# Residual rows issued by ScalarE, the output projection placed after the last attention slot, and transposing loads spread out, in an attention and FFN layer on 8 cores

## The chip, the cores and the metric

The kernel is one program on all 8 cores of one Trainium2 chip. Time is device microseconds (us) of the slowest core. Each core has the matrix engine (TensorE, PE in the profile), VectorE (DVE), ScalarE (ACT), GpSimd (POOL) and SyncE (SP), which each run their own instruction stream in order, and issue DMAs in that same order. They meet by semaphores.

## The reference

For 4 sequences of 4096 tokens and 2048 features, two post-norm steps (cut to what matters):

```python
# attention: tokens of a sequence are seen as 2 batches of 2048, 16 heads of 128
mixed = x @ Wqkv.T                       # q, k, v
attn = softmax((q @ k.T) / sqrt(128))
out = (attn @ v) @ Wproj.T + bproj
x = layernorm(x + out)                   # called h1 in the kernel
# feed-forward: weights packed in 4 bits, with a scale for each group of 128 inputs
gate, up = x @ w_gate.T, x @ w_up.T
y = (silu(gate) * up) @ w_down.T
x = layernorm(x + y / sqrt(mean(y * y) + 1e-6))
```

## The kernel before

Each core computes 2048 output tokens of one sequence, in 16 tiles of 128 tokens.

Attention runs in 8 slots of 128 steps. In a step TensorE computes the scores of 256 keys for 512 queries (`pe_scores`, 2 matmuls of 512 columns), ScalarE exponentiates them (`act_exp`, one instruction of 1024 columns), and TensorE multiplies an earlier result with V (`pe_context`, 8 matmuls of 129 columns). Every 16 steps VectorE normalizes and evacuates the context (`dve_ctx_evac`), during which the next context matmul waits. Between scores and context `pe_program` puts filler: in slots 0 to 6 five projection matmuls' worth of the next slot, and in slot 7, from step `OC_FIRST = 60` on, five matmuls of the output projection (`pe_out_proj`). The rest of the output projection follows behind attention.

The output projection has 64 groups (16 tiles by 4 blocks of 512 columns) of 16 matmuls. Group q is written to one of two PSUM banks, and waits for VectorE's evacuation of group q-2. The work on a tile goes round several engines:

- SP loads the tile's context transposed (`sp_ctx_load`) and the residual rows `xr` (`sp_xr_load`, 1 MB, two buffers: tile t+2 takes the buffer of tile t).
- POOL adds the bias to `xr` (`pool_bias`), VectorE adds `xr` to the projection for each group, with statistics (`dve_post_norm`: `r`, `statB`, `aggB`), POOL turns the variance into `rstdB` (`pool_rstd_b`), and VectorE writes `h1f`.
- POOL stores `h1f`, ScalarE casts it to `h1b` (`act_h1_cast`) and stores that.

POOL's stream is written out in a fixed order, which the change leaves alone:

```python
    for tile in range(TILES):
        pool_rstd_b(g, S, M, tile)
        g.wait_ge(S.h1_done, tile + 1)
        g.dma_start(out=M.d_h1[tile * 128:(tile + 1) * 128, :],
                    in_=M.h1f[tile % 2][:]).then_inc(S.h1_stored[tile % 2], 16)
        if tile + 2 < TILES:
            pool_bias(g, S, M, tile + 2)
```

The feed-forward part takes 4 chunks of 512 tokens. A chunk has 44 gate/up operations (`pe_gate_up`, 32 matmuls each) on transposed `h1T`, and 4 x 11 blocks of the down projection. SP feeds it: `sp_wgu_load` fetches weights into a ring of 4 (1 MB each; the load of operation k waits until operation k-4 is done), and at operation 10 of a chunk `sp_h1t_load` fetches the next chunk's four tiles with four transposing loads in a row.

Of the kernel before, what the change touches and what calls it, by code (L numbers as in the profile page):

```python
# [543 lines left out]
def act_program(a, S, M, exact):  # L544
    a.wait_ge(S.consts, 1)
    g = 0
    while g < GROUPS:
        act_proj_evac(a, S, M, g)
        g += 1
    tile = 0  # L550
    for n in range(SLOTS * STEPS):
        act_exp(a, S, M, n)
        last = n % STEPS == STEPS - 1
        while g < groups_done(n if exact and last else n - 1):
            act_proj_evac(a, S, M, g)
            g += 1
        if n >= (SLOTS - 1) * STEPS and 4 * (tile + 1) <= oc_groups_done(n % STEPS - 5):
            act_h1_cast(a, S, M, tile)
            tile += 1
    while tile < TILES:  # L560
        act_h1_cast(a, S, M, tile)
        tile += 1

    for ch in range(FCH):
        for op in range(GU_OPS):
            act_silu(a, S, M, ch * GU_OPS + op)
        for oc in range(4 if ch + 1 < FCH else 3):
# [4 lines left out]
    a.wait_ge(S.l_norm, 12)
    a.wait_ge(S.l_done, 4)
    a.dma_start(out=M.d_out[r * 128:(r + 1) * 128, 1024:2048],
                in_=M.res[3][:, 1024:2048]).then_inc(S.out_last[1], 16)
# [525 lines left out]
                          ).then_inc(S.ctxt_in[tile % CTXT_RING], 16)  # L1101


def sp_xr_load(y, S, M, tile):
    if tile >= 2:
        y.wait_ge(S.oc_evac, 4 * (tile - 1))
    y.dma_start(out=M.xr[tile % 2][:],
                in_=M.d_xrows[tile * 128:(tile + 1) * 128, :]).then_inc(S.xr_in[tile % 2], 16)


def sp_h1t_load(y, S, M, ch, tiles):
    if ch >= 2:
# [27 lines left out]
def sp_program(y, S, M, exact):  # L1140
# [10 lines left out]
    if exact:  # L1151
        sp_row_max(y, S, M, SLOTS - 1)
    y.wait_ge(S.pv_done, (SLOTS - 1) * STEPS)
    sp_xr_load(y, S, M, 0)
    sp_xr_load(y, S, M, 1)
    xr = ctxt = 0
    for i in range(STEPS):
        if i % 16 == 15:
            sp_ctx_store(y, S, M, (SLOTS - 1) * QBLOCKS + i // 16)
        if i == 34:  # L1160
            y.wait_ge(S.proj_done, SLOTS * GROUPS)
            while ctxt < CTXT_RING:
                sp_ctx_load(y, S, M, ctxt)
                ctxt += 1
        if 4 * (xr + 1) <= oc_groups_done(i - 2):
            sp_xr_load(y, S, M, xr + 2)
            xr += 1
        while ctxt - CTXT_RING < xr and 32 * (ctxt // 4 + 1) <= i:
            sp_ctx_load(y, S, M, ctxt)
            ctxt += 1  # L1170
    y.wait_ge(S.pv_done, SLOTS * STEPS)
    for j in range(2):
        y.wait_ge(S.ctx_stored[j], 16 * (SLOTS * QBLOCKS // 2))
    while xr + 2 < TILES:
        if xr == TILES - 5:
            sp_wgu_load(y, S, M, 0)
            sp_wgu_load(y, S, M, 1)
        if xr >= TILES - 4:
            sp_h1t_load(y, S, M, 0, range(2 * (xr - TILES + 4), 2 * (xr - TILES + 4) + 2))
        while ctxt < TILES and ctxt - CTXT_RING <= xr:  # L1180
            sp_ctx_load(y, S, M, ctxt)
            ctxt += 1
        sp_xr_load(y, S, M, xr + 2)
        xr += 1
    sp_wgu_load(y, S, M, 2)
    sp_wgu_load(y, S, M, 3)
    for ch in range(FCH):
        for op in range(GU_OPS):
            kc = ch * GU_OPS + op + WGU_RING
            if kc < FCH * GU_OPS:  # L1190
                sp_wgu_load(y, S, M, kc)
            if op == 10 and ch + 1 < FCH:
                sp_h1t_load(y, S, M, ch + 1, range(4))
            if op == 34 and ch == 0:
                for du in range(WD_RING):
                    sp_wd_load(y, S, M, du)
# [157 lines left out]
```

## Time and profile before

| what | us |
| --- | --- |
| median of 3 runs (lowest, highest) | 4144.91 (4142.04, 4147.2) |
| the profiled execution, time | 4153.74 |
| its span (slowest core, core 2) | 4152.0 |
| spans of all cores | 4127.6 to 4152.0 |
| TensorE busy in the span | 4060.1 (98%) |
| mean granted TensorE clock of the cores | 0.996 to 0.999 |

The profile is of one execution, on its slowest core. Rows of a timeline give start, duration, engine, line and operation; in brackets stands the idle time before the instruction and what ended it. Rows with SPq, ACTq or POOLq, and POOL's DMA rows, are the issue of a DMA, not its transfer.

### The profile page before, as it was taken

The page shows a single profiled execution, that of the slowest core. Times are in us where ns is not written, and L with a number is a line of the kernel's source. Part 1 is how long each engine was busy: PE and PEld are TensorE (multiplying, and loading weights), DVE is VectorE, ACT ScalarE, POOL GpSimd, SP SyncE. Part 2 cuts the span into 40 slices and gives each one's busy share as a digit, 9 for nine tenths or more (in the row PEclk, how much of TensorE's full clock was granted, in tenths as well). Part 3 has the DMA queues.
Part 4 walks back from the last instruction along what each step waited for, and adds up shares of the span by engine and source line. Part 5 has one row for each costly group of instructions (what it writes and reads, how often), then busy time and mean ns, then how long its engine had stood idle before and what let it go on. Part 6 is the DMA issues. An engine that isn't in the chain of part 4 may idle for free.

```text
span 4152.0 us, 66120 instructions; the slowest of 8 cores (4127.6 to 4152.0 us)
## 1 busy us (share of the span) xinstructions
PE 4060.1 (98%) x26491; PEld 2296.5 (55%) x26881; DVE 948.6 (23%) x1433; ACT 1400.2 (34%) x1610; POOL 286.4 (7%) x434
## 2 busy tenths in 40 slices
PE   7999999999999999999999999999999999999998
PEld 4666666666666766666554444444444444444443
DVE  0054452222222223220234100022100300022124
ACT  1355555555555555557642100000000000000001
POOL 1100000000000000000223000000000000000000
PEclk9999999999999999999999999999999999999999
DMA  9777776465655655656459545447444654446433
GB/s 146 130 172 169 178 165 126 107 137 121 124 119 118 140 104 120 135 119 111 110 157 261 191 167 199 159 155 231 152 157 152 201 189 152 157 164 216 162 127 123
DMA packets 251041, 635.65 MB, mean 153 GB/s; under 512 B 115184, under 2 KB 137712, under 8 KB 212720
## 3 DMA queue, kind: packets, MB, share of 16 engines
q1 hardware_dynamic: 202496, 426.29, 31.6%
q0 software_dynamic: 45792, 196.10, 25.5%
q10 hardware_dynamic: 2448, 8.91, 0.5%
q8 instruction: 225, 3.69, 0.4%
q14 instruction: 80, 0.66, 0.0%
HBM read 643.83 MB, written 119.54 MB: 184 GB/s over the span
## 4 chain that ended last, share of the span: by engine, by line
PE 93%; SPq 2%; DMA 2%; issue 1%; ACT 1%; DVE 0%; POOL 0%; ACTq 0%; DVEq 0%; POOLq 0%
PE pJ L283 16%; PE pC L339 11%; PE pJ L269 11%; PE pS L320 10%; PE pS L412 7%; PE pS L393 7%; PE pS L389 7%; PE pC L389 4%; PE pJ L393 3%; PE pC L393 3%; PE pJ L389 3%; PE pJ L361 3%; PE pC L412 3%; PE pJ L412 3%; SPq L1118 2%
## 5 line engine op out<-in xcount | busy, mean ns | idle before, releaser
L496 ACT ACTIVATE P<-pS 128x1024 bf16<-128x1024 f32 x1024 | 1027.8, 1026 | 356.8 <-PE pS L320 342.6
L283 PE MATMUL pJ<-x,wq 128*128 128x512 bf16 x2984 | 756.9, 381 | 28.5 <-DMA x<-xc 23.8
L339 PEld LDWEIGHTS pC<-V,P 128*128 128x128 bf16 x8192 | 549.8, 98 | 168.0 <-issue 11.3
L339 PE MATMUL pC<-V,P 128*128 128x129 bf16 x8192 | 634.0, 220 | 3.6 <-DVE ctxg L613 3.1
L320 PE MATMUL pS<-Q,K 128*128 128x512 bf16 x1829 | 561.7, 379 | 18.9 <-ACT P L496 7.5
L269 PE MATMUL pJ<-wq,x 128*128 128x256 bf16 x4096 | 514.8, 273 | 0.4
L283 PEld LDWEIGHTS pJ<-x,wq 128*128 128x128 bf16 x3072 | 301.0, 98 | 381.9 <-issue 33.4
L269 PEld LDWEIGHTS pJ<-wq,x 128*128 128x128 bf16 x4096 | 400.7, 98 | 134.8
L609 DVE RECIPROCAL rcp<-pC 128x4 f32<-128x4 f32 x64 | 11.7, 183 | 1477.9 <-PE pC L339 1477.9
L393 PE MATMUL pS<-h1T,wgu 128*128 128x512 bf16 x1408 | 318.3, 379 | 0.0
L389 PE MATMUL pS<-h1T,wgu 128*128 128x512 bf16 x1408 | 318.3, 379 | 0.0
L412 PE MATMUL pS<-wd,hffnT 128*128 128x512 bf16 x1380 | 303.1, 379 | 1.5
L905 POOL DMA_DIRECT2D x<-xc x256 | 138.3, 558 | 1743.6 <-PE pJ L283 1089.0
L361 PE MATMUL pJ<-wp,ctxT 128*128 128x512 bf16 x1001 | 232.8, 380 | 9.1 <-DVE r L674 7.8
L517 ACT ACTIVATE sg<-pS 128x512 bf16<-128x512 f32 x88 | 52.4, 597 | 532.5 <-PE pS L389 532.5
L389 PEld LDWEIGHTS pS<-h1T,wgu 128*128 128x128 bf16 x1408 | 137.9, 98 | 166.0
L412 PEld LDWEIGHTS pS<-wd,hffnT 128*128 128x128 bf16 x1408 | 137.8, 98 | 166.1
L393 PEld LDWEIGHTS pS<-h1T,wgu 128*128 128x128 bf16 x1408 | 137.8, 98 | 166.1
L389 PE MATMUL pC<-h1T,wgu 128*128 128x512 bf16 x704 | 163.5, 386 | 13.5 <-DMA wgu<-wgu_scr 13.5
L695 DVE TENSOR_TENSOR hffnT<-sg,pS 128x512 bf16<-128x512 bf16 x88 | 60.6, 688 | 498.6 <-PE pS L393 492.1
L361 PEld LDWEIGHTS pJ<-wp,ctxT 128*128 128x128 bf16 x1024 | 100.0, 98 | 129.7 <-issue 11.4
L320 PEld LDWEIGHTS pS<-Q,K 128*128 128x128 bf16 x2048 | 157.0, 98 | 11.5 <-issue 8.4
(107 smaller groups left out, 2647.8 us busy)
## 6 DMA issues: line engine op xcount, KB each, us to landing
wgu<-wgu_scr SPq DMA_DIRECT2D x176, 1024.0 KB, 4.9
x<-xc POOLq DMA_DIRECT2D x256, 512.0 KB, 12.4
wd<-wdn_scr SPq DMA_DIRECT2D x174, 512.0 KB, 3.5
wgu_scr<-bits SPq DMA_DIRECT2D x44, 1024.0 KB, 5.1
wdn_scr<-bits SPq DMA_DIRECT2D x44, 512.0 KB, 4.6
xr<-xrows SPq DMA_DIRECT2D x16, 1024.0 KB, 7.1
h_scr<-h1f POOLq DMA_DIRECT2D x16, 1024.0 KB, 7.1
res<-h_scr POOLq DMA_DIRECT2D x16, 1024.0 KB, 8.9
```

What stands on the lines that cost most here:

```text
L269: mm = t.matmul(out[:, tt * 256:(tt + 1) * 256], x[:, hc, (2 * h + tt) * 128:(2 * h + tt + 1) * 128], M.wq[:, pair, 1, hc, :], start=(hc = ...
L283: mm = t.matmul(out, M.wq[:, pair, part, hc, h * 128:(h + 1) * 128], x[:, hc, :], start=(hc == 0), stop=(hc == HC - 1))
L320: mm = t.matmul(M.pS[n % 2][:, h * 512:(h + 1) * 512], M.K[s % 2][:, l, kt * 128:(kt + 1) * 128], M.Q[s % 2][:, l, qc * 512:(qc + 1) * 512 ...
L339: mm = t.matmul(M.pC[:, o:o + 129], M.P[n % 3][:, h * 512 + qt * 128:h * 512 + (qt + 1) * 128], M.V[s % 2][:, 2 * p + h, l, :], start=(p = ...
L361: mm = t.matmul(M.bank(6 + q % 2), M.ctxT[tile % CTXT_RING][:, hc, :], M.wp[2 * oc + hc // 8][:, hc % 8, :], start=(hc == 0), stop=(hc == ...
L389: mm = t.matmul(M.bank(b), w[:, kt % 4, kt // 4, 0:128], M.h1T[ch % 2][:, :, kt, :], start=(kt == 0), stop=(kt == HC - 1))
L393: mm = t.matmul(M.bank(b + 1), w[:, kt % 4, kt // 4, 128:256], M.h1T[ch % 2][:, :, kt, :], start=(kt == 0), stop=(kt == HC - 1))
L412: mm = t.matmul(M.bank((oc % 2) * 4 + tt), M.hffnT[:, 4 * ut + j, tt * 128:(tt + 1) * 128], M.wd[du % WD_RING][:, j, :], start=(ut == 0 an ...
L496: a.activation(out=M.P[n % 3][:], in_=M.pS[n % 2][:], func=AF.Exp, bias=0.0, scale=NORM).then_inc(S.exp_done, 1)
L695: v.tensor_tensor(out=M.hffnT[:, kc % GU_OPS, :], in0=M.sg[kc % 2][:], in1=M.bank(PAIR_BANKS[kc % 4] + 1), op=ALU.mult).then_inc(S.h_done, 1)
L905: g.dma_start(out=M.x[gc % 2][:, 4 * q:4 * q + 4, :], in_=M.d_x[w, ch, :, 4 * q:4 * q + 4, :]).then_inc(S.x_in[(gc % 2) * 4 + q], 16)
L1118: y.dma_start_transpose(out=M.h1T[ch % 2][:, tt, :, :], in_=M.d_h1b[tile * 128:(tile + 1) * 128, :]).then_inc(S.h1t_in[ch % 2], 16)
```

## The change

Four edits:

- `OC_FIRST` becomes 128, so slot 7 has no filler and all 64 groups of the output projection follow attention.
- The residual rows of tiles 2 to 15 are no longer issued by SP but by ScalarE, at the end of `act_h1_cast` of the tile two before.
- The cast of `h1b` is four instructions of 512 columns in place of one of 2048.
- The four transposing loads of the next chunk's `h1T` are issued at operations 8, 15, 22 and 29, one each, in place of four at operation 10.

```diff
-OC_FIRST = 60
+OC_FIRST = STEPS
...
+H1T_OPS = (8, 15, 22, 29)
...
-def act_h1_cast(a, S, M, tile):
+def act_h1_cast(a, S, M, k):
...
+    tile, ut = divmod(k, 4)
+    cols = slice(512 * ut, 512 * (ut + 1))
     a.wait_ge(S.h1_done, tile + 1)
     if tile >= 2:
         a.wait_ge(S.h1b_stored[tile % 2], 16 * (tile // 2))
-    a.copy(out=M.h1b[tile % 2][:].rearrange("t (u j p) -> t u j p", u=4, j=4),
-           in_=M.h1f[tile % 2][:].rearrange("t (u p j) -> t u j p", u=4, j=4)
-           ).then_inc(S.h1b_done, 1)
+    cast = a.copy(out=M.h1b[tile % 2][:, cols].rearrange("t (j p) -> t j p", j=4),
+                  in_=M.h1f[tile % 2][:, cols].rearrange("t (p j) -> t j p", j=4))
+    if ut < 3:
+        return
+    cast.then_inc(S.h1b_done, 1)
     a.wait_ge(S.h1b_done, tile + 1)
     a.dma_start(out=M.d_h1b[tile * 128:(tile + 1) * 128, :],
                 in_=M.h1b[tile % 2][:]).then_inc(S.h1b_stored[tile % 2], 16)
+    if tile + 2 < TILES:
+        a.wait_ge(S.oc_evac, 4 * (tile + 1))
+        a.dma_start(out=M.xr[tile % 2][:], in_=M.d_xrows[(tile + 2) * 128:(tile + 3) * 128, :]
+                    ).then_inc(S.xr_in[tile % 2], 16)
...
-        if n >= (SLOTS - 1) * STEPS and 4 * (tile + 1) <= oc_groups_done(n % STEPS - 5):
-            act_h1_cast(a, S, M, tile)
-            tile += 1
-    while tile < TILES:
-        act_h1_cast(a, S, M, tile)
-        tile += 1
+        if n >= (SLOTS - 1) * STEPS and 4 * (k // 4 + 1) <= oc_groups_done(n % STEPS - 5):
+            act_h1_cast(a, S, M, k)
+            k += 1
+    for k in range(k, 4 * TILES):
+        act_h1_cast(a, S, M, k)
...
-def sp_xr_load(y, S, M, tile):
-    if tile >= 2:
-        y.wait_ge(S.oc_evac, 4 * (tile - 1))
-    y.dma_start(out=M.xr[tile % 2][:],
-                in_=M.d_xrows[tile * 128:(tile + 1) * 128, :]).then_inc(S.xr_in[tile % 2], 16)
...
-            if op == 10 and ch + 1 < FCH:
-                sp_h1t_load(y, S, M, ch + 1, range(4))
+            if op in H1T_OPS and ch + 1 < FCH:
+                tt = H1T_OPS.index(op)
+                sp_h1t_load(y, S, M, ch + 1, range(tt, tt + 1))
```

TensorE's stream in slot 7, before (a step late in the slot; pS are scores, pC the context, pJ the output projection):

```order
L339 MATMUL pC<-V_100,P_140 128x129 x8
L320 MATMUL pS<-Q_102,K_98 128x512 x2
L361 MATMUL pJ<-wp_82,ctxT_83 128x512 x5
L339 MATMUL pC<-V_100,P_141 128x129 x8
L320 MATMUL pS<-Q_102,K_98 128x512 x2
L361 MATMUL pJ<-wp_75,ctxT_84 128x512 x5
```

And changed, at the end of the slot:

```order
L321 MATMUL pS<-Q_102,K_98 128x512 x2
L340 MATMUL pC<-V_100,P_140 128x129 x8
L340 MATMUL pC<-V_100,P_141 128x129 x8
L340 MATMUL pC<-V_100,P_139 128x129 x8
L362 MATMUL pJ<-wp_75,ctxT_83 128x512 x8
L362 MATMUL pJ<-wp_76,ctxT_83 128x512 x8
L362 MATMUL pJ<-wp_77,ctxT_83 128x512 x8
```

The pJ matmuls are gone from between scores and context; the first of them follows the last context matmuls.

ScalarE's stream behind attention, before (P is the last exponential, h1b the cast rows):

```order
L496 ACTIVATE P_139<-pS 128x1024
L505 CAST h1b_123<-h1f_106 128x2048
L509 DMA h1b_scr<-h1b_123 128x2048
L505 CAST h1b_124<-h1f_107 128x2048
L509 DMA h1b_scr<-h1b_124 128x2048
```

Changed:

```order
L497 ACTIVATE P_139<-pS 128x1024
L509 CAST h1b_123<-h1f_106 128x512 x4
L515 DMA h1b_scr<-h1b_123 128x2048
L519 DMA xr_103<-xrows 128x2048
L509 CAST h1b_124<-h1f_107 128x512 x4
L515 DMA h1b_scr<-h1b_124 128x2048
L519 DMA xr_104<-xrows 128x2048
```

Each residual load now stands behind the four casts and the store of the tile two before it.

SP's stream near the end of the output projection, before (ctxT and h1T are transposing loads, wgu the first weights of the feed-forward part):

```order
L1107 DMA xr_103<-xrows 128x2048
L1126 DMA wgu_112<-wgu_scr 128x4096
L1126 DMA wgu_113<-wgu_scr 128x4096
L1099 DMA_TRANSPOSE ctxT_86<-ctx_scr 128x16x128
L1107 DMA xr_104<-xrows 128x2048
L1118 DMA_TRANSPOSE h1T_126<-h1b_scr 128x16x128 x2
L1107 DMA xr_103<-xrows 128x2048
L1118 DMA_TRANSPOSE h1T_126<-h1b_scr 128x16x128 x2
L1107 DMA xr_104<-xrows 128x2048
```

Changed:

```order
L1108 DMA_TRANSPOSE ctxT_85<-ctx_scr 128x16x128
L1128 DMA wgu_112<-wgu_scr 128x4096
L1128 DMA wgu_113<-wgu_scr 128x4096
L1108 DMA_TRANSPOSE ctxT_86<-ctx_scr 128x16x128
L1120 DMA_TRANSPOSE h1T_126<-h1b_scr 128x16x128 x4
L1128 DMA wgu_114<-wgu_scr 128x4096
L1128 DMA wgu_115<-wgu_scr 128x4096
```

The residual loads are gone from SP, and the four transposing loads of the first chunk stand together. The streams of POOL and VectorE have the same instructions in the same order around the output projection in both kernels.

## Rows read from the trace of the kernel before

**Rows 1.** Timeline, VectorE in slot 7: start, duration, what [idle before, releaser].
```profile
1937.73 0.18 DVE L609 RECIPROCAL rcp<-pC 128x4 f32<-128x4 f32 x1 [30.64 <-PE pC L339]
...
1954.13 0.18 DVE L609 RECIPROCAL rcp<-pC 128x4 f32<-128x4 f32 x1 [15.41 <-PE pC L339]
...
1986.37 0.18 DVE L609 RECIPROCAL rcp<-pC 128x4 f32<-128x4 f32 x1 [15.14 <-PE pC L339]
...
2138.38 0.18 DVE L609 RECIPROCAL rcp<-pC 128x4 f32<-128x4 f32 x1 [2.94 <-PE pC L339]
```

**Rows 2.** Busy time (x count) of PE, PEld, DVE, ACT, POOL; clock; DMA share; GB/s.
```profile
2139.30:2295.40 156.10, 147.48 (x668) 66.50 (x680) 76.35 (x112) 39.23 (x11) 57.42 (x40) 0.99 0.79 234
```

**Rows 3.** Timeline, TensorE at the end of the output projection.
```profile
2287.11 2.72 PE L361 MATMUL pJ<-wp,ctxT 128*128 128x512 bf16 x6 [3.29 <-DVE r L674]
2289.99 5.56 PE L361 MATMUL pJ<-wp,ctxT 128*128 128x512 bf16 x25 [0.17 <-issue]
2295.39 3.62 PE L389 MATMUL pS<-h1T,wgu 128*128 128x512 bf16 x16
```

**Rows 4.** The chain that ended last, one transfer: start, duration.
```profile
2269.55 9.54 DMA xr<-xrows
```

**Rows 5.** Timeline, POOL near the end of the output projection.
```profile
2279.23 4.50 POOL L918 TENSOR_TENSOR xr<-xr,bias 128x2048 f32<-128x2048 f32 x1 [9.94 <-DMA xr<-xrows]
2283.71 0.22 POOL L928 TENSOR_SCALAR epsB<-aggB 128x1 f32<-128x1 f32 x1
```

**Rows 6.** Timeline, VectorE behind attention.
```profile
2147.90 0.69 DVE L674 TENSOR_TENSOR r<-pJ,xr 128x512 f32<-128x512 f32 x1 [1.99 <-PE pJ L361]
...
2151.09 1.34 DVE L687 TENSOR_SCALAR h1f<-r,aggB,rstdB 128x2048 f32<-128x2048 f32 x1 [1.33 <-POOL rstdB L931]
...
2284.75 1.34 DVE L687 TENSOR_SCALAR h1f<-r,aggB,rstdB 128x2048 f32<-128x2048 f32 x1 [5.87 <-POOL rstdB L931]
```

**Rows 7.** Timeline, TensorE in chunks 1 and 2 of the feed-forward part.
```profile
2847.92 3.62 PE L389 MATMUL pJ<-h1T,wgu 128*128 128x512 bf16 x16
2851.37 3.62 PE L393 MATMUL pJ<-h1T,wgu 128*128 128x512 bf16 x16
2862.06 5.93 PE L389 MATMUL pC<-h1T,wgu 128*128 128x512 bf16 x16 [7.07 <-DMA wgu<-wgu_scr]
2867.83 3.62 PE L393 MATMUL pC<-h1T,wgu 128*128 128x512 bf16 x16
...
3326.85 5.65 PE L389 MATMUL pC<-h1T,wgu 128*128 128x512 bf16 x16 [6.47 <-DMA wgu<-wgu_scr]
```

**Rows 8.** Timeline, SP's issues behind attention and in chunk 1.
```profile
2233.26 6.24 SPq L1099 DMA_TRANSPOSE ctxT<-ctx_scr  x1
...
2827.96 22.47 SPq L1118 DMA_TRANSPOSE h1T<-h1b_scr  x4
```

**Rows 9.** Timeline, TensorE in slot 7 behind a cast on ScalarE.
```profile
2035.66 0.59 PE L320 MATMUL pS<-Q,K 128*128 128x512 bf16 x2 [1.34 <-ACT P L496]
```

**Rows 10.** Timeline, ScalarE behind attention.
```profile
2152.57 3.90 ACT L505 CAST h1b<-h1f 128x2048 bf16<-128x2048 f32 x1 [13.08 <-DVE h1f L687]
2156.55 0.34 ACTq L509 DMA_DIRECT2D h1b_scr<-h1b  x1
```

**Rows 11.** Tile xr within slot 7 (1990 to 2140).
```profile
DMA to landing us min/median/max: 5.2/5.4/5.4
```

**Rows 12.** Tile xr behind attention (2140 to 2300).
```profile
DMA to landing us min/median/max: 6.4/7.8/9.7
```

**Rows 13.** DMA issues from 2820 to 2870: KB each, median us to landing.
```profile
wgu<-wgu_scr SPq DMA_DIRECT2D x6, 1024.0 KB, 12.4
```

**Rows 14.** What line L389 waited for on core 7: us, times.
```profile
  DMA wgu<-wgu_scr: 3.8, 1
```

**Rows 15.** Spans and mean granted clock, two of the cores.
```profile
core 2: 4152.0 us, clock 0.996
...
core 7: 4139.8 us, clock 0.998
```

More of the change, by code:

```diff
@@ L549, in act_program @@
         g += 1
-    tile = 0
+    k = 0
     for n in range(SLOTS * STEPS):
@@ L1153, in sp_program @@
     y.wait_ge(S.pv_done, (SLOTS - 1) * STEPS)
-    sp_xr_load(y, S, M, 0)
-    sp_xr_load(y, S, M, 1)
-    xr = ctxt = 0
+    for tile in range(2):
+        y.dma_start(out=M.xr[tile][:],
+                    in_=M.d_xrows[tile * 128:(tile + 1) * 128, :]).then_inc(S.xr_in[tile], 16)
+    done = ctxt = 0
     for i in range(STEPS):
@@ L1164, in sp_program @@
                 ctxt += 1
[L1165 to L1168, printed above, removed]
+        if 4 * (done + 1) <= oc_groups_done(i - 2):
+            done += 1
+        while ctxt - CTXT_RING < done and 32 * (ctxt // 4 + 1) <= i:
             sp_ctx_load(y, S, M, ctxt)
@@ L1173, in sp_program @@
         y.wait_ge(S.ctx_stored[j], 16 * (SLOTS * QBLOCKS // 2))
-    while xr + 2 < TILES:
-        if xr == TILES - 5:
+    for tile in range(done, TILES - 2):
+        if tile == TILES - 5:
             sp_wgu_load(y, S, M, 0)
             sp_wgu_load(y, S, M, 1)
-        if xr >= TILES - 4:
-            sp_h1t_load(y, S, M, 0, range(2 * (xr - TILES + 4), 2 * (xr - TILES + 4) + 2))
-        while ctxt < TILES and ctxt - CTXT_RING <= xr:
+        if tile >= TILES - 4:
+            tt = 2 * (tile - TILES + 4)
+            sp_h1t_load(y, S, M, 0, range(tt, tt + 2))
+        while ctxt < TILES and ctxt - CTXT_RING <= tile:
             sp_ctx_load(y, S, M, ctxt)
             ctxt += 1
-        sp_xr_load(y, S, M, xr + 2)
-        xr += 1
     sp_wgu_load(y, S, M, 2)
```

## The prediction

> **What bounds the kernel now.** The busy times say TensorE, nearly everywhere. So I read the list of waits only to find where TensorE waits, and then timelines there. Three places matter. In slot 7 before the filler begins, ScalarE's exponentials set the pace: VectorE's context evacuations, one for every 16 steps, stand 16.40 us and then 32.24 / 2 = 16.12 us apart [rows 1], about 1.007 us a step. Behind attention TensorE is busy 147.5 of 156.1 us [rows 2]; the rest is three waits for VectorE, the last one 3.29 us [rows 3]. That one goes back to residual rows that landed late: the load took 9.54 us [rows 4], POOL stood idle 9.94 us for it [rows 5], and VectorE then waited 5.87 us for POOL's rstdB [rows 6]. In the feed-forward part core 2 waits twice for weights, 7.07 and 6.47 us [rows 7], behind four transposing loads that hold SP for 22.47 us [rows 8].
>
> **Part 1, filler out of slot 7.** From the first evacuation of the slot to the last it takes 2138.38 - 1937.73 = 200.65 us [rows 1]. Without filler all eight stretches go at ScalarE's pace: 16.40 + 7 x 16.12 = 129.24 us. Attention ends 71.4 us earlier, near 2066.8. This holds already that ScalarE no longer stops for casts between exponentials, each of which cost TensorE at least the 1.34 us of [rows 9] and happened four times.
>
> All 64 groups now follow. A group is 16 matmuls of 512 columns; 16 such matmuls follow the last 16 after 2851.37 - 2847.92 = 3.45 us when nothing waits [rows 7], so unhindered they take 64 x 3.45 = 221 us and end at 2287.8, against 2295.4 now [rows 3]: 7.6 us earlier. This is the best that Parts 1 and 2 could give.
>
> **Part 2, residual rows behind the cast.** This is where I expect the loss. The load of xr for tile t+2 used to need only the evacuation of tile t's last group, and SP's queue; now it stands behind h1f of tile t and four casts on ScalarE. And POOL's stream has the bias addition of tile t+2 ahead of rstdB of tile t+1. POOL works in order: at 2283.71 epsB starts the moment the bias addition ends, and VectorE's h1f follows [rows 5, 6]. Before, that was a wait now and then. In the changed kernel it closes a loop of one tile: h1f(t), cast, load of xr(t+2), bias(t+2), rstdB(t+1), h1f(t+1). Its length L, from start of h1f to start of the next h1f:
>
> - start of h1f to start of the cast: 2152.57 - 2151.09 = 1.48 us [rows 6, 10];
> - the cast, 3.90 us [rows 10]; in four pieces I take 4.2. Four pieces do not exist before. From below it is 3.9; from above I allow another 0.3 us a piece, 5.1; I stay close to the row, since the elements are the same;
> - to the issue of xr: 0.08 + 0.34 for the h1b store [rows 10] + 0.08 = 0.50 us;
> - D, the load from issue to landing, see below;
> - landing (2269.55 + 9.54 = 2279.09) to bias start 0.14 us [rows 4, 5];
> - bias start to h1f start: 2284.75 - 2279.23 = 5.52 us [rows 5, 6].
>
> L = 11.84 + D. The loop hides behind TensorE only if it is no longer than a tile's 4 x 3.45 = 13.8 us, that is with D under 2.0 us. D was 5.2 to 5.4 us with little traffic [rows 11] and 6.4 to 9.7 us behind attention [rows 12]. Those are the two ends, 5.2 and 9.7. In the change the transposing load that preceded xr in SP's queue (6.24 us of issue, [rows 8]) no longer precedes it, but the h1b store, half as large as xr, does; a store of h1f is in flight too. I take 6.5 us: 5.2 plus a quarter, for half as many bytes ahead of which part is done in the time of the issue. So L = 18.3 us, 4.5 us longer than a tile.
>
> The rows say that the load slowed from 5.4 to 7.8 us in the median when other traffic grew, both times in SP's queue [rows 11, 12]. The Trainium skill says the same in "DMA: Bandwidth & Descriptors", section "Issuing engines are not separate DMA queues": DMAs started by different engines run on the same 16 DMA engines and interleave, so another issuer saves only issue time. That rule speaks against this edit: it would not let D fall under the 5.2 us of a quiet stretch (about 4170 in all), while a queue with transfers of its own would. No run so far shows this load on ScalarE's queue.
>
> Now the sum. The first tile ends 13.8 us after 2066.8, at 2080.6. h1f(0) starts 2151.09 - 2147.90 = 3.2 us later [rows 6], at 2083.8. The loop turns 14 times (loads of tiles 2 to 15): 14 x 18.34 = 256.8, so h1f(14) starts at 2340.6. The last two loads meet the feed-forward weights and the four transposing loads that now stand together on SP; the load in such a stretch took 9.54 us [rows 4]. I add 3 and 2 us: 2345.6. TensorE restarts 2287.11 - 2284.75 = 2.36 us after h1f's start and does two groups in 2295.39 - 2287.11 = 8.28 us [rows 3, 6]; that is 1.4 us over 2 x 3.45, as the first matmuls after a wait run at the lower clock. The output projection ends at 2356.2, against 2295.4: **60.8 us later**. In the other turns these 1.4 to 2.3 us at the lower clock [rows 3, 7] fit into the 4.5 us that TensorE is ahead of the loop, and cost nothing. The casts are ahead of nothing else on ScalarE.
>
> **Part 3, transposing loads spread.** Matmul group starts are 2867.83 - 2851.37 = 16.46 us apart across the first wait where 6.9 is normal: 9.6 us, of which 2.3 are the lower clock. The second: 6.47 + (5.65 - 3.62) = 8.5 us [rows 7]. Together 18.1 us on core 2. One transposing load alone takes about 22.47 / 4 = 5.6 us of SP [rows 8]. A weight load is issued four operations ahead, so three operations, 20.7 us, cover it; 5.6 us leave 15 of them, more than a load needed even in the crowd (the median of the weight loads there was 12.4 us [rows 13]). So these waits go. On core 7 there is only one wait, 3.8 us [rows 14], perhaps 5 with the clock. If cover were gone, a late load costs what it costs now.
>
> **Sum.** Core 2: 4152.0 + 60.8 - 18.1 = 4194.7. Core 7: 4139.8 + 60.8 - 5 = 4195.6 [rows 15]. Both are near 4195, and with the 1.7 us outside the span of the profiled execution 4197. The runs' median is 8.8 us below the profiled one, which had core 2's long waits; core 7 alone would give 4139.8 + 1.7 = 4141.5 [rows 15]. On the median: 4144.9 + 60.8 - 18.1 = 4187.6, or with core 7's gain 4200.7. I take **4193**.
>
> **Rivals.**
>
> A. *The residual chain has two tiles of time, not one.* xr has two buffers, and the load serves tile t+2. Were it not for POOL's order, the chain would only need to bring xr(t+2) in time for its first group: 3.2 + 1.48 + 4.2 + 0.5 + 6.5 + 0.14 + 4.5 + 0.7 = 21.2 us after tile t's last group, where 6 groups, 20.7 us, are free. TensorE would wait about 0.5 us per pair of tiles, 4 us in all, and the change gives -7.6 + 4 - 5 to -18.1: **about 4130, faster**. It decides from the point where rstdB(t+1) does not wait for xr(t+2). Against it: epsB right behind the bias addition [rows 5].
>
> B. *The loop turns faster*, D = 5.2, as in a quiet stretch: 14 x 1.3 + 5 = 23 us less, 4170. For it: traffic per us falls as tiles take longer. Against: h1b's store directly ahead.
>
> C. *The load is slow throughout*, D near 9.7: 14 x 3.2 less the 5 already counted, about 40 us more, 4233. For it: the maximum of [rows 12] on an ordinary tile. Against: it needs transposing loads in front each time.
>
> D. *Spreading does not stop the waits for weights.* One transposing load among fast-running loads still delays one. The 5 to 18 us are then not gained: 4198 to 4211.
>
> **How the numbers follow.** My forecast, the loop at L of 17.8 to 19.5 us, 58%, by itself 4183 to 4210. A 6%, B 18%, C 8%, D together with the loop 10%. The range 4163 to 4225 holds B, the forecast and D, and leaves out A and C. A measurement of this kernel tells a change from none at about 0.2%, 8 us. Faster: A alone, 0.06; the same, the tail of B in which D is near 4 us, 0.02; slower 0.92.
>
> **What would show it.** Right: VectorE's h1f starts 18 to 19 us apart behind attention, TensorE waits for `r` about 4.5 us in nearly every tile, POOL waits for xr in every tile and epsB starts at the end of the bias addition; slot 7 takes about 129 us; no wait of TensorE for wgu. Wrong: h1f starts 13.8 us apart, or POOL's waits for xr ending before aggB is there. The sum fails in proportion if D is not 6.5 us: each us is 14 us of time.

## The result, and the profile after

| what | predicted | measured |
| --- | --- | --- |
| ratio to before | 1.0116 (4193) | 1.0158 [1.0135, 1.0181] |
| time, us | 4193 (4163 to 4225) | 4144.91 x 1.0158 = 4210; runs of 4205.6 to 4212.7 |

The change makes the kernel slower by 1.6%, 65 us where I had forecast 48. The profiled execution (core 1, span 4488.1 us) had a granted TensorE clock of 0.81 to 0.91 in most of slots 0 to 6 and 1.00 just before slot 7, so only stretches from slot 7 on are compared. A second profile of the same kernel (core 7, span 4214.7 us, time 4216.46) gives whole spans.

**Slot 7.** VectorE's context evacuations, as in [rows 1]:

```profile
2226.31 0.18 DVE L618 RECIPROCAL rcp<-pC 128x4 f32<-128x4 f32 x1 [30.64 <-PE pC L340]
2242.71 0.18 DVE L618 RECIPROCAL rcp<-pC 128x4 f32<-128x4 f32 x1 [15.42 <-PE pC L340]
...
2355.36 0.18 DVE L618 RECIPROCAL rcp<-pC 128x4 f32<-128x4 f32 x1 [14.72 <-PE pC L340]
```

From the first to the last that is 129.05 us in place of 200.65.

**Output projection.** The three stretches slot 7, output projection and feed-forward, in the columns of [rows 2]:

```profile
2226.00:2355.00 129.00, 122.11 (x1279) 83.66 (x1277) 7.00 (x16) 122.21 (x128) 11.65 (x7) 1.00 0.43 83
2355.00:2653.40 298.40, 243.26 (x1047) 104.85 (x1045) 113.79 (x167) 62.24 (x60) 85.10 (x61) 0.93 0.58 172
2653.40:4488.00 1834.60, 1819.88 (x8432) 824.85 (x8430) 298.64 (x477) 154.62 (x253) 43.82 (x93) 1.00 0.51 172
```

Only in the middle one is TensorE far from busy: 243 of 298 us, at a mean clock of 0.93. Its waits there, as a timeline (compare [rows 3]):

```profile
2394.96 15.99 PE L362 MATMUL pJ<-wp,ctxT 128*128 128x512 bf16 x64 [5.15 <-DVE r L683]
2413.13 13.97 PE L362 MATMUL pJ<-wp,ctxT 128*128 128x512 bf16 x64 [2.18 <-DVE r L683]
2431.66 16.41 PE L362 MATMUL pJ<-wp,ctxT 128*128 128x512 bf16 x64 [4.55 <-DVE r L683]
...
2605.83 16.36 PE L362 MATMUL pJ<-wp,ctxT 128*128 128x512 bf16 x64 [9.91 <-DVE r L683]
...
2641.17 8.75 PE L362 MATMUL pJ<-wp,ctxT 128*128 128x512 bf16 x32 [3.97 <-DVE r L683]
2649.76 3.62 PE L390 MATMUL pS<-h1T,wgu 128*128 128x512 bf16 x16
```

From the second tile on, each tile's 64 matmuls are followed by a wait, 14 waits in all. After waits of 1.0 to 3.8 us five of these pieces take 13.97 us; after waits of 2.3 to 9.9 us eight take 15.3 to 16.4. They are the same 64 matmuls, part of them at the lower clock: the granted clock is 1.00 over the piece that starts at 2413.13 and 0.85 over the one at 2431.66. One turn of the loop, VectorE and POOL (compare [rows 5, 6]):

```profile
2392.61 1.34 DVE L696 TENSOR_SCALAR h1f<-r,aggB,rstdB 128x2048 f32<-128x2048 f32 x1 [7.74 <-POOL rstdB L940]
...
2410.78 1.35 DVE L696 TENSOR_SCALAR h1f<-r,aggB,rstdB 128x2048 f32<-128x2048 f32 x1 [4.77 <-POOL rstdB L940]
```

```profile
2405.25 4.51 POOL L927 TENSOR_TENSOR xr<-xr,bias 128x2048 f32<-128x2048 f32 x1 [10.09 <-DMA xr<-xrows]
2409.73 0.22 POOL L937 TENSOR_SCALAR epsB<-aggB 128x1 f32<-128x1 f32 x1
2410.10 0.57 POOL L940 TENSOR_TENSOR rstdB<-epsB,powB 128x1 f32<-128x1 f32 x1
```

And ScalarE between them (compare [rows 10]):

```profile
2394.04 4.13 ACT L509 CAST h1b<-h1f 128x512 bf16<-128x512 f32 x4 [16.13 <-DVE h1f L696]
2398.25 0.34 ACTq L515 DMA_DIRECT2D h1b_scr<-h1b  x1
2398.68 0.76 ACTq L519 DMA_DIRECT2D xr<-xrows  x1
```

Read round: h1f 2392.61, casts 2394.04, load issued 2398.68, bias addition 2405.25, epsB right behind it, next h1f 2410.78. The sums over the whole kernel, from the list of waits (total us, times, longest):

```profile
POOL xr L927 <- DMA xr<-xrows: 190.2, 15, 36.8
...
DVE h1f L696 <- POOL rstdB L940: 93.6, 16, 12.5
...
PE pJ L362 <- DVE r L683: 55.1, 14, 9.9
```

Before, the last was 7.8 us in 3 waits. TensorE has no wait for wgu any more on any core (compare [rows 7, 14]). The landing of xr from 2300 to 2700 (compare [rows 12]):

```profile
DMA to landing us min/median/max: 5.6/6.8/12.1
```

In the second profile all eight cores show 14 waits for `r`, 52.3 to 64.3 us each. One turn there lasted 30.26 us (core 7, VectorE, and what SP issued in it):

```profile
2297.89 1.35 DVE L696 TENSOR_SCALAR h1f<-r,aggB,rstdB 128x2048 f32<-128x2048 f32 x1 [7.53 <-POOL rstdB L940]
...
2328.15 1.35 DVE L696 TENSOR_SCALAR h1f<-r,aggB,rstdB 128x2048 f32<-128x2048 f32 x1 [17.34 <-POOL rstdB L940]
```

```profile
2271.79 1.03 SPq L1128 DMA_DIRECT2D wgu<-wgu_scr  x2
2288.49 3.90 SPq L1108 DMA_TRANSPOSE ctxT<-ctx_scr  x1
2292.54 27.41 SPq L1120 DMA_TRANSPOSE h1T<-h1b_scr  x4
```

The residual load issued at 2304.01, in the middle of four transposing loads, took 18.5 us to land. The same turn, the twelfth, is the longest on every core of both profiles, 21.9 to 33.7 us.

### The profile page after: what moved, and what is told of

Read it like the earlier page. It is cut to its first block, busy times and chain, and to the rows that moved or that the text cites. A ratio compares the mean times of both kernels' runs of the same rounds, so it can differ in the third digit from the quotient of the medians.

```text
span 4488.1 us, 66672 instructions; the slowest of 8 cores (4455.6 to 4488.1 us)
## 1 busy us (share of the span) xinstructions
PE 4387.7 (98%) x26881; PEld 2424.4 (54%) x26881; DVE 947.8 (21%) x1433; ACT 1405.7 (31%) x1658; POOL 286.2 (6%) x434
## 4 chain that ended last, share of the span: by engine, by line
PE 92%; DMA 3%; issue 2%; ACT 2%; DVE 1%; POOL 1%; ACTq 0%; POOLq 0%; DVEq 0%
PE pJ L284 17%; PE pJ L270 12%; PE pC L340 11%; PE pS L321 11%; PE pS L394 7%; PE pS L413 7%; PE pS L390 7%; PE pJ L390 3%; PE pC L394 3%; PE pC L390 3%; PE pJ L394 3%; PE pJ L413 3%; PE pC L413 3%; DMA xr<-xrows 2%; ACT h1b L509 1%
## 5 line engine op out<-in xcount | busy, mean ns | idle before, releaser
L284 PE MATMUL pJ<-x,wq 128*128 128x512 bf16 x3072 | 876.4, 424 | 22.7 <-DMA x<-xc 22.7
L340 PEld LDWEIGHTS pC<-V,P 128*128 128x128 bf16 x8192 | 602.2, 105 | 205.9 <-issue 131.4
L340 PE MATMUL pC<-V,P 128*128 128x129 bf16 x8192 | 692.0, 233 | 6.6 <-DVE ctxg L622 6.1
L321 PE MATMUL pS<-Q,K 128*128 128x512 bf16 x2048 | 676.6, 416 | 1.1 <-ACT P L497 1.1
L270 PE MATMUL pJ<-wq,x 128*128 128x256 bf16 x4096 | 587.2, 298 | 0.0
L284 PEld LDWEIGHTS pJ<-x,wq 128*128 128x128 bf16 x3072 | 326.7, 106 | 461.1 <-issue 375.5
L270 PEld LDWEIGHTS pJ<-wq,x 128*128 128x128 bf16 x4096 | 435.0, 106 | 184.8 <-issue 93.8
L321 PEld LDWEIGHTS pS<-Q,K 128*128 128x128 bf16 x2048 | 168.6, 104 | 8.5 <-issue 2.3
L490 ACT CAST V<-pJ 128x512 bf16<-128x512 f32 x128 | 75.4, 589 | 274.2 <-PE pJ L270 274.2
```

Of the source, the lines that this page charges most:

```text
L270: mm = t.matmul(out[:, tt * 256:(tt + 1) * 256], x[:, hc, (2 * h + tt) * 128:(2 * h + tt + 1) * 128], M.wq[:, pair, 1, hc, :], start=(hc = ...
L284: mm = t.matmul(out, M.wq[:, pair, part, hc, h * 128:(h + 1) * 128], x[:, hc, :], start=(hc == 0), stop=(hc == HC - 1))
L321: mm = t.matmul(M.pS[n % 2][:, h * 512:(h + 1) * 512], M.K[s % 2][:, l, kt * 128:(kt + 1) * 128], M.Q[s % 2][:, l, qc * 512:(qc + 1) * 512 ...
L340: mm = t.matmul(M.pC[:, o:o + 129], M.P[n % 3][:, h * 512 + qt * 128:h * 512 + (qt + 1) * 128], M.V[s % 2][:, 2 * p + h, l, :], start=(p = ...
L490: a.copy(out=out, in_=bank).then_inc(S.proj_evac, 1)
```

## The experiments

Theory: the loop h1f, cast, load, bias, rstdB sets the pace of the output projection because the load stands behind the cast on ScalarE; the other edits are worth little. Rivals: it is POOL's order alone; it is the placement of the output projection; it is traffic on the DMA engines. The kernels ran in three sets (1 to 4; 5, 6, 7 and 11; 8, 9, 10 and 12), each beside the kernel before, whose median was 4152.0, 4155.4 and 4154.1 us. Ratios are to it, with a 95% interval. D is the time of the residual load from issue to landing, as in the prediction. Where one time stands, there was one run to compare.

| kernel | times, us | ratio, where there were runs enough |
| --- | --- | --- |
| 1 changed, xr issued by SP again | 4135.9 to 4145.3 | 0.9963 [0.9940, 0.9986] |
| 2 changed, POOL's bias addition later | 4197.3, 4201.1 | |
| 3 changed, xr issued ahead of the casts | 4157.7, 4177.6 | |
| 4 changed, xr ahead of the wait for h1f | 4199.9, 4213.9 | |
| 5 as 3, SP paced by tile | 4156.4 | |
| 6 before, loads spread | 4137.7 to 4143.8 | 0.9964 [0.9946, 0.9981] |
| 7 before, output projection behind attention | 4148.4 | |
| 8 before, cast in quarters (four of 512 columns) | 4156.8 | |
| 9 changed, OC_FIRST = 60 | 4182.1 | |
| 10 changed, again | 4216.5 | |
| 11 best of the parts, xr first on SP | 4138.3, 4138.7 | |
| 12 as 11, weights behind the last xr | 4124.7 to 4143.7 | 0.9948 [0.9920, 0.9976] |

**1. One edit undone.** The three other edits stay.

```diff
-    if tile + 2 < TILES:          # at the end of act_h1_cast
-        a.wait_ge(S.oc_evac, 4 * (tile + 1))
-        a.dma_start(out=M.xr[tile % 2][:], ...)
...
         if 4 * (done + 1) <= oc_groups_done(i - 2):
+            sp_xr_load(y, S, M, done + 2)
...
+        sp_xr_load(y, S, M, tile + 2)    # last in SP's loop over tiles
```

> The changed kernel, with the residual rows issued by SP again, behind each tile's context load; the three other edits stay. Loop theory (the cast and the load of xr stand in a chain of one tile's length with POOL's bias addition and rstdB): the load leaves 4.7 us after the last group instead of behind h1f and the cast, so nearly all of the loss goes: output projection 221 to 232 us in place of 294.6, time about 4130 to 4142. Rival (the loss comes from taking the filler out of slot 7, or from the four joined transposing loads): stays above 4190.

Measured: median 4140.2. TensorE's end of the output projection on the slowest core:

```profile
2258.76 29.47 PE L362 MATMUL pJ<-wp,ctxT 128*128 128x512 bf16 x128 [4.04 <-DVE r L679]
2292.53 8.75 PE L362 MATMUL pJ<-wp,ctxT 128*128 128x512 bf16 x32 [4.30 <-DVE r L679]
2301.12 3.62 PE L390 MATMUL pS<-h1T,wgu 128*128 128x512 bf16 x16
```

Two waits in place of 14; h1f stands 13.8 us apart in most tiles. One edit carries the loss: 4210 - 4140 = 70 us, or 81 by the two ratios, which were taken in different sets. The cores say about 70: from the last evacuation to the first gate matmul the eight take 223.6 to 232.8 us here, and 294.6 to 306.6 in the second profile of the change. What remains of the change is a small gain. POOL's order is the same here, and the output projection is in the same place: alone neither costs this.

**2. POOL's order.** The bias addition for tile t+1 goes behind rstdB of tile t, so rstdB no longer waits for a load.

```diff
         pool_rstd_b(g, S, M, tile)
+        if 2 <= tile + 1 < TILES:
+            pool_bias(g, S, M, tile + 1)
         g.wait_ge(S.h1_done, tile + 1)
...
-        if tile + 2 < TILES:
-            pool_bias(g, S, M, tile + 2)
```

> The changed kernel, with one move in POOL's stream: the bias addition of tile t+1 stands between rstdB of tile t and the store of h1f of tile t, instead of the one of tile t+2 behind that store. The load of xr stays on ScalarE behind the casts. Loop theory: rstdB no longer waits for xr, so the chain has two tiles of time; the bias is then ready some 8.1 us after a tile's last group, where 6.9 are free, so 1 to 3 us a tile remain: output projection 240 to 265 us, time 4150 to 4180. Rival (the load itself is late, whatever POOL's order): h1f stays 19 us apart and the time within 10 us of the changed kernel.

Measured: 4197 and 4201, and a miss. The median core has a span of 4182 us, 21 less than in the second profile of the change, but core 0, the slowest, has 4199 because one load took 27.3 us. The intended wait is gone, but something else came (VectorE and POOL, core 0):

```profile
2134.87 1.35 DVE L696 TENSOR_SCALAR h1f<-r,aggB,rstdB 128x2048 f32<-128x2048 f32 x1 [1.34 <-POOL rstdB L940]
...
2173.24 5.45 DVE L696 TENSOR_SCALAR h1f<-r,aggB,rstdB 128x2048 f32<-128x2048 f32 x1 [1.34 <-POOL rstdB L940]
```

```profile
2173.11 4.49 POOL L927 TENSOR_TENSOR xr<-xr,bias 128x2048 f32<-128x2048 f32 x1
```

VectorE idles only 1.34 us before h1f, but where POOL's addition starts first, the same h1f takes 5.45 us instead of 1.35: it ends 1.1 us after the addition does (2178.69 against 2177.60), as if it had stood still until then. The Trainium skill has this in "SBUF — State Buffer", section "SBUF: two separate sides": GpSimd and VectorE, in some of its operations, share a pair of ports as an exclusive lock; the instruction that starts first has it to its end, and the other one blocks. The trace agrees to 0.3 us (1.35 us behind the addition's end would be 2178.95).

This happens in 6 to 10 of the 16 tiles of a core. On core 6 it is every second one from tile 2 to tile 8, and in those between the addition itself is late, for its load was issued behind the slow h1f:

```profile
2146.71 5.46 DVE L696 TENSOR_SCALAR h1f<-r,aggB,rstdB 128x2048 f32<-128x2048 f32 x1 [1.33 <-POOL rstdB L940]
...
2169.69 0.69 DVE L683 TENSOR_TENSOR r<-pJ,xr 128x512 f32<-128x512 f32 x1 [4.79 <-POOL xr L927]
...
2180.89 5.46 DVE L696 TENSOR_SCALAR h1f<-r,aggB,rstdB 128x2048 f32<-128x2048 f32 x1 [1.34 <-POOL rstdB L940]
```

So the loop now runs over two tiles, 34.2 us here, 17.1 a tile in place of 18 to 20 in the change. Taking POOL's order away was worth about 2 us a tile. Without the 4.1 us that h1f stood still, the same loop would take 30.1 us, 15.0 a tile (an estimate): still over 13.8. Every core still shows 14 waits for `r`, 43 to 62 us in all.

**3. The load ahead of the casts.** It still waits for h1f(t) on ScalarE, but not for the casts and the store.

```diff
     a.wait_ge(S.h1_done, tile + 1)
+    if ut == 0 and tile + 2 < TILES:
+        a.wait_ge(S.oc_evac, 4 * (tile + 1))
+        a.dma_start(out=M.xr[tile % 2][:], ...)
```

> The changed kernel, with the load of xr issued by ScalarE after it has waited for h1f but ahead of the four casts and of the h1b store. Loop theory: the loop is shorter by 4.2 + 0.5 us and by what the h1b store ahead costs the load: L = 1.5 + 0.1 + D (5.5 to 6.5) + 0.1 + 5.5 = 12.7 to 13.7, about a tile's 13.8 us; output projection 221 to 235 us, time 4130 to 4145. Rival (ScalarE's queue is a slow place for this load): D stays 6.8 or more and L near 14.5, time 4145 to 4155.

Measured: 4157.7 and 4177.6, so faster than the change, but by less than expected. The second time is that of core 2, and some 25 us of it are not the loop's: on cores 2 and 3 the feed-forward part took 1864 us in place of 1838.5, at a granted clock of 0.95 in its first part. Core 6, with 4170.0, has no such stretch. By the loop's terms a turn is 1.5 + D + 0.14 + 5.5, with the median D of 6.6 us 13.7, under the 13.8 of a tile; and eight turns in a row on core 0 are 13.8 us apart (2111.03 to 2221.91 is 110.9). The rest is in single loads near the end. Core 6, VectorE, and SP's issues there:

```profile
2223.75 1.34 DVE L696 TENSOR_SCALAR h1f<-r,aggB,rstdB 128x2048 f32<-128x2048 f32 x1 [1.70 <-POOL rstdB L940]
...
2246.10 1.35 DVE L696 TENSOR_SCALAR h1f<-r,aggB,rstdB 128x2048 f32<-128x2048 f32 x1 [10.23 <-POOL rstdB L940]
...
2291.13 1.34 DVE L696 TENSOR_SCALAR h1f<-r,aggB,rstdB 128x2048 f32<-128x2048 f32 x1 [30.91 <-POOL rstdB L940]
```

```profile
2240.79 45.69 SPq L1120 DMA_TRANSPOSE h1T<-h1b_scr  x4
```

The load issued at 2247.58, beside these four, landed after 37.9 us. The loop's arithmetic is confirmed, and there is a second term: single loads on ScalarE's queue are late when SP has much under way. The one before, issued at 2225.23 right behind SP's first two weight loads and followed by a transposing load, took 15.2 us.

**4. The load ahead of the wait for h1f.** The same block one line higher, so it waits for the last evacuation alone, as SP's load did.

```diff
+    if ut == 0 and tile + 2 < TILES:
+        a.wait_ge(S.oc_evac, 4 * (tile + 1))
+        a.dma_start(out=M.xr[tile % 2][:], ...)
     a.wait_ge(S.h1_done, tile + 1)
```

> As before this one, but ScalarE issues the load of xr without waiting for h1f: it waits only for the evacuation of the tile's last group. Loop theory: the load is out of the loop, leaves 0.8 us after a tile's last group, and POOL has its bias done before rstdB is wanted: output projection 221 to 225 us, no wait of TensorE for r over 1 us, time 4125 to 4137 (-7.6 us of slot 7 and tail, -5 to -13 us of the feed-forward waits). Rival (the early load now meets the context transposes on the DMA engines): D 8 to 10 us, some waits of 1 to 3 us, 4135 to 4150.

Measured: 4199.9 and 4213.9, a large miss. The load no longer waits for anything but its buffer, and the cores fall apart: 4128.6 us on core 2, 4198.2 on core 1. Landing of xr behind attention, core 2 first, then core 1:

```profile
DMA to landing us min/median/max: 6.3/7.8/13.1
```

```profile
DMA to landing us min/median/max: 9.6/21.4/29.7
```

On core 1 SP's transposing loads of ctxT take 28.0 us in the median as well (8.6 on core 2), and TensorE waits 60.2 us for `r`. Kernel 1 issues the same loads at the same condition, from SP, and has a median of 7.0 us. So a free instruction stream is not enough. On core 1, one such load in the chain that ended last, and what SP issued 0.8 us before it:

```profile
2134.28 28.46 DMA xr<-xrows
```

```profile
2133.48 10.52 SPq L1108 DMA_TRANSPOSE ctxT<-ctx_scr  x1
```

The residual load is released by a tile's last evacuation and the ctxT load by its last matmul, so on two queues they run side by side; on SP's alone they took turns. Which resource they fight for, and why only on some cores, stays open.

**5. Pacing SP.** Kernel 3, and SP waits at the end of each tile's loads.

```diff
             ctxt += 1
+        y.wait_ge(S.oc_evac, 4 * (tile + 1))
```

> The changed kernel with xr issued by ScalarE behind its wait for h1f but ahead of the casts (as the third kernel of the first set), and SP made to wait at the end of each tile's loads for the tile's last evacuation, so that the first chunk's four transposing loads are again issued two a tile. In the earlier kernel h1f stood 13.8 us apart for eleven tiles, then 20 to 45 us once, with xr landing after 14 to 38 us, when wgu and four transposing loads were in flight. Theory (bunched loads from SP's queue starve the load in ScalarE's queue): the longest landing falls under 12 us on every core and the single long wait shrinks to under 4 us. Rival (any transposing load in flight from the other queue can starve it): landings of 14 us and more stay on some cores.

Measured: 4156.4. The latest load still took 14.1 to 15.7 us on seven cores and 26.0 on core 5, so SP running ahead of the tiles does not make all of the late loads. On most cores the one that remains is that behind the two weight loads, which the pacing does not touch. Whether there the weights or the transposing load behind them are the cause, no kernel tells; in number 4 the slow loads begin before any weight load.

**6, 7, 8. Each other part alone, on the kernel before.**

```diff
-            if op == 10 and ch + 1 < FCH:          # 6
-                sp_h1t_load(y, S, M, ch + 1, range(4))
+            if op in H1T_OPS and ch + 1 < FCH:
+                tt = H1T_OPS.index(op)
+                sp_h1t_load(y, S, M, ch + 1, range(tt, tt + 1))
...
-OC_FIRST = 60                                     # 7
+OC_FIRST = STEPS
...
-def act_h1_cast(a, S, M, tile):                   # 8, with its calls
+def act_h1_cast(a, S, M, k):
```

> The kernel before with one edit alone: the transposing loads of the next chunk at operations 8, 15, 22 and 29. Theory: TensorE's waits for wgu (13.5 us on core 2 of the first profile, 2.7 to 10 us on the others) and the 2 us of lower clock behind each go; nothing else moves. Time 4 to 13 us less, 4134 to 4142. Rival (one transposing load among weight loads still delays one): waits for wgu remain, spread over more operations, time within 4 us of before.

> The kernel before with OC_FIRST = 128 alone. Theory: slot 7 takes 129 us in place of 200.7, all 64 groups follow in 221 us plus the waits for xr behind SP's transposing loads, which now can come in 14 tiles and not only in 9: 5 to 14 us of waits. Output projection 226 to 235 us; span 2 us less to 7 us more than before. Rival (taking the filler out is the loss): first context evacuation of slot 7 to the first gate matmul takes 400 us or more, in place of 357.7.

> The kernel before with the cast in quarters alone (filler in slot 7 as before). Theory: one quarter a step lies in the 0.9 us that ScalarE waits for scores in a step with filler, so TensorE's waits for P behind casts (7 us with what PE's record hides, 1.9 us the longest) go: slot 7 takes 195 us in place of 200.7. Rival: a quarter of 1.05 us still pushes the exponential, slot 7 stays over 199 us.

Measured. 6: no core waits for wgu in the feed-forward part; 0.9964 of 4155 us is a gain of 15 us [8, 22], close to the 5 to 18 us of Part 3. 7: from slot 7's first evacuation to the first gate matmul 356.4 us (core 5), against 2295.39 - 1937.73 = 357.7 before [rows 1, 3]; over the eight cores 351.9 to 357.9 against 351.2 to 358.0. Moving the output projection behind attention is worth about nothing by itself. 8: slot 7 took

```profile
1942.31 0.18 DVE L612 RECIPROCAL rcp<-pC 128x4 f32<-128x4 f32 x1 [30.64 <-PE pC L339]
...
2136.51 0.18 DVE L612 RECIPROCAL rcp<-pC 128x4 f32<-128x4 f32 x1 [2.94 <-PE pC L339]
```

194.2 us, against 200.65. The quarters save 6.4 us there: TensorE waits 0.2 to 0.6 us for P in that slot, in place of 6.0 to 6.7. They can do so only while slot 7 holds filler and casts, and the change takes both out. In that one run the slowest core's other waits (`r` 12.9 us, wgu 11.3) took the gain back.

**9. The change with filler in slot 7.**

```diff
-OC_FIRST = STEPS
+OC_FIRST = 60
```

> The changed kernel with OC_FIRST = 60 again: filler in slot 7 as before, the other three edits stay, xr on ScalarE behind the casts. Theory (one loop turn costs 18.9 us against 13.8, wherever it is bound by the loop): in slot 7 tiles are 27 us apart, so the loop is hidden there; behind attention it turns 9 to 10 times, 5.2 us over each: tail 50 us longer than in the kernel before, less 5 us of casts and 4 to 13 us of weight waits. Span 4170 to 4185. Rival (the output projection behind attention, not the loop, is the loss): under 4150.

Measured: 4182.1, as the loop theory had it. Behind attention the same loop turns (here a few tiles later than in the profile of the change):

```profile
2170.68 15.36 PE L362 MATMUL pJ<-wp,ctxT 128*128 128x512 bf16 x64 [5.61 <-DVE r L683]
2189.27 15.66 PE L362 MATMUL pJ<-wp,ctxT 128*128 128x512 bf16 x64 [3.24 <-DVE r L683]
```

18.6 us a tile, 9 or 10 waits in place of 14, and 34 us less than the change in the same set (number 10). The tiles that go as filler in slot 7 are slower than the loop anyway and hide it; putting all of them behind attention exposes all 14 turns.

**10. The change again**, for whole spans; its rows are above.

> The changed kernel itself once more, beside the others. From its first trace: h1f 19.0 us apart behind attention, output projection 294.6 us, slot 7 129 us, no wait for wgu. The same numbers within 3 us; span 4195 to 4215. If the loop were an accident of the one profiled execution, the output projection would be under 280 us on some cores.

Measured: 4216.5. The loop is there on all eight cores, so it is no accident of one execution. But the same numbers within 3 us did not come: the output projection took 294.6 to 306.6 us by core, with the slowest core at the upper end.

**11 and 12. Towards a better kernel.** Number 11 keeps the filler, takes quarters and spread, and puts xr first among SP's loads of a tile. Number 12 also moves the feed-forward part's first weights behind the last xr, and the first chunk's transposing loads, one a tile, to tiles 7 to 10.

```diff
     while xr + 2 < TILES:
+        sp_xr_load(y, S, M, xr + 2)              # 11 and 12
-        if xr == TILES - 5:                      # 12
-            sp_wgu_load(y, S, M, 0)
-            sp_wgu_load(y, S, M, 1)
-        if xr >= TILES - 4:
-            sp_h1t_load(y, S, M, 0, range(2 * (xr - TILES + 4), 2 * (xr - TILES + 4) + 2))
+        if TILES - 9 <= xr < TILES - 5:
+            sp_h1t_load(y, S, M, 0, range(xr - TILES + 9, xr - TILES + 10))
...
-        sp_xr_load(y, S, M, xr + 2)
...
+    for kc in range(WGU_RING):
+        sp_wgu_load(y, S, M, kc)
```

> A version meant to be faster than both: filler in slot 7 as before, casts in quarters, transposing loads spread, and the residual rows issued by SP, behind attention ahead of the tile's other loads instead of behind them. Expected against before: casts between exponentials no longer stop TensorE (4 x 1.3 us), waits for xr behind attention gone (2.2 to 8 us and their lower clock), waits for wgu gone (4 to 13 us): 12 to 24 us less, 4121 to 4133 where before has 4145, D of xr 5.2 to 6.5 us behind attention. Rival (xr ahead delays the context or h1T loads so that TensorE waits for those): waits for ctxT or h1T appear, gain under 10 us.

> The version of the last set (filler in slot 7, casts in quarters, spread loads, xr ahead of SP's other loads) with two more moves on SP: the first chunk's four transposing loads one a tile, four tiles earlier, and all four first weight loads (1 MB each) behind the last xr. In the last version the transposing load right behind two weight loads held SP for 14 to 16 us, the next ones 26 us, and one xr came 16 us too late on core 3. Theory (bunched SP loads near the end of the output projection are what is left): waits of TensorE for r and h1T under 2 us on every core, cores' spans 4115 to 4130, ratio to before 0.992 to 0.995. Rival (the weights now come too late): TensorE waits 2 us or more for wgu at the first gate matmul, no gain over the last version.

Measured. 11: 4138.3 and 4138.7, over the times expected. Against the 4155.4 of its set that is 17 us less, inside the 12 to 24, but the waits for xr are not gone. Seven cores were at 4120 to 4131, but core 3 had one wait of 16.4 us for `r`, and cores 1 and 5 waited 3.2 and 5.5 us for h1T. SP's issues on core 3:

```profile
2225.31 0.90 SPq L1130 DMA_DIRECT2D wgu<-wgu_scr  x2
2226.41 14.20 SPq L1103 DMA_TRANSPOSE ctxT<-ctx_scr  x1
2240.71 0.51 SPq L1111 DMA_DIRECT2D xr<-xrows  x1
2241.37 26.16 SPq L1122 DMA_TRANSPOSE h1T<-h1b_scr  x2
2267.64 0.50 SPq L1111 DMA_DIRECT2D xr<-xrows  x1
```

A transposing load issued 0.2 us behind two weight loads of 1 MB holds SP for 14.2 us, two more for 26.2, and the next xr waits in line. In the kernel before the same weight loads stood ahead of the 6.24 us of [rows 8], but 8 us earlier:

```profile
2223.03 2.00 SPq L1126 DMA_DIRECT2D wgu<-wgu_scr  x2
```

Number 12 takes the weight loads out of this place and spreads the transposing loads. TensorE then waits for neither `r`, h1T nor wgu on seven cores. The one wait on the slowest core (3.6 us, where under 2 was expected), and its landing of xr behind attention there:

```profile
2240.56 50.19 PE L362 MATMUL pJ<-wp,ctxT 128*128 128x512 bf16 x224 [3.59 <-DVE r L678]
2290.59 3.62 PE L390 MATMUL pS<-h1T,wgu 128*128 128x512 bf16 x16
```

```profile
DMA to landing us min/median/max: 5.9/7.2/10.7
```

Cores 4117.7 to 4129.0, median of six runs 4128.8, ratio 0.9948 [0.9920, 0.9976]: 0.5% faster than the kernel before, and faster than the change. It is not told apart from numbers 1 and 6, whose intervals overlap with its own.

## Why the prediction was right in kind and short in size

The time 4210 lies in the range, and the forecast of the likeliest case missed by 17 us. It lies in the band of rival D as well, 4198 to 4211, so the time alone could not tell the two; the terms can:

| term | predicted | measured (first / second profile) |
| --- | --- | --- |
| slot 7 | 129.24 us | 129.05 / 129.0 |
| h1f to cast | 1.48 | 1.43 / 1.49 |
| cast in four | 4.2 | 4.13 / 4.12 |
| to the issue | 0.50 | 0.51 / 0.51 |
| D, median | 6.5 | 6.8 / 7.4 |
| bias start to h1f | 5.52 | 5.53 / 5.51 |
| a turn, mean | 18.3 | 19.0 / 19.9 |
| last evacuation to first gate matmul | 289.4 | 294.4 / 306.6 |
| feed-forward: core 2's 1856.6 less 18.1 | 1838.5 | 1838.3 (core 1) / 1838.6 (core 7) |

**The mechanism** was as written. The loop has the members named, it turns 14 times, and kernel 1 shows that the place of the load makes it. Rival A, two tiles of time per load, is refuted by the profile: epsB stands right behind the bias addition in every turn. But its price was wrong too: kernel 2 took the order away and gave the load its two tiles, and TensorE still waited in every tile, since h1f took 5.46 us in many tiles, beside POOL's addition, and D was 7.2 to 8.4 us in the median. I had weighed POOL's order as a wait only, not what its instruction does to its neighbour.

**The term that was mis-sized is D.** In the second profile all is there to add up: h1f(0) to h1f(14) took 278.1 us, where I had 14 x 18.34 + 5 = 261.8. That is 16.3 of the 17.2 us by which this stretch was longer: 9.4 in thirteen turns of 19.06 us in the mean, 6.9 in the one of 30.26. The mean turn, 19.0 and 19.9 us in the two profiles, lies at and beyond the end of the 17.8 to 19.5 that I had forecast. The mean turn of 19.86 less 11.76 for all but D makes D 8.1 us. Its median was 7.4, 0.9 more than my "5.2 plus a quarter", and one load took 18.5 us. I had allowed 5 us in all for the crowd at the end, from a load that took 9.54 us in SP's own queue [rows 4]; on ScalarE's queue, beside the four transposing loads that the change itself puts together, it was worse: 12.1, 18.5, and 37.9 in kernel 3. The 9.54 us were measured in the other queue, and I used them as a bound without saying so. As a bound for the median, 9.7 held in every run where the load still waited for h1f; for a single load it did not. In both profiles of the changed kernel no load of xr behind attention landed under 5.4 us, on any core. The rule that I had cited from the Trainium skill, "DMA: Bandwidth & Descriptors", section "Issuing engines are not separate DMA queues", is borne out so far: another issuer brought no faster load. That it can bring a much slower one, as in kernel 4, no sentence of mine allowed for.

**The gain of Part 3** was right: 18.1 us on core 2, 15 us [8, 22] on the median alone. In the second profile the eight cores take 1838.4 to 1839.0 us for this part; before it was 1841.5 to 1856.6, so the gain is 3 to 18 us by core. Rival D is refuted, no core waits for wgu. I had taken a mean of about 13 us into the sum.

**Part 1** was right for slot 7, and its 7.6 us for the best case were never there. They set a stretch without waits against core 2's, which had 7.8 us of waits for `r`; in kernel 7 such waits stay, 2.0 to 5.3 us a core. Number 12 shows what the filler is worth with the quarters: 194.2 us in slot 7 and 147.4 behind it on seven cores, 341.6 in all, where without filler 129.0 + 221 = 350 is the best. With the loop turning, the move costs more: numbers 9 and 10 differ by 34 us in single runs, for the filler had hidden four of the turns and the quarters had been worth 6.4 us with it.

**The rest of the sum.** Second profile against the forecast of 4195 for a span: 4214.7 is 19.7 us more, 2.5 of it because slot 7 began and so ended later on that core, 17.2 in the output projection, none in the feed-forward part. Two slips in the sums are small beside this: attention ends at 2138.38 - 71.41 = 2067.0, not 2066.8, and a turn of 17.8 us gives 4185, not 4183.

Open: which resource makes a plain load on ScalarE's queue and transposing loads on SP's slow each other, and why by core. The weight loads are a third suspect for the late loads near the end. A kernel with the residual loads in a third queue was not tried.

## What to carry to other kernels

Before a load is moved to another engine, write down what that engine has in front of it and follow the ring back to the load: with two buffers and an in-order engine in it that also serves the next tile, the ring has one tile of time, not two. In this kernel it was best to keep the load that something waits for in the same queue as the transposing loads, ahead of them, and the bulk prefetches behind the last of it (number 12). And run the parts of a mixed change alone: here one edit cost 70 to 80 us and hid another that was worth 15.

## What the runs showed of the hardware that I had not expected

- VectorE's 128x2048 f32 h1f: 1.35 us alone, 5.45 us when POOL's 128x2048 f32 addition had started 0.13 us before it.
- The residual load of 1 MB issued on ScalarE's queue: in both profiles of the change and in kernel 3, median 6.2 to 7.4 us by core, with single loads of 10 to 38 us when SP had weight or transposing loads under way; started together with them, 21.4 us in the median on one core and 7.8 on another of the same run.
- A transposing load 0.2 us behind two 1 MB weight loads held SP for 13.3 to 16.7 us on the eight cores of kernel 11; 8 us behind them, in the kernel before, for 6.24 [rows 8]. Four of them in a row on SP took 14.0, 27.4 and 45.7 us in three profiles.
